# Gated graph kernel on one core: hx and h0 turned feature-major by a DMA trip and 32x32 vector transposes, scores from unsplit fp32

## What is computed

```python
h = jnp.maximum(_layernorm(x, axis=-1), 0.0)
x = x + _L0_gnn_ref(h, adj, Wq, Wk, Wv)        # q k^T, times adj^T, over its row norm, times v
h = jnp.maximum(_layernorm(x, axis=-1), 0.0)
# layer 1, three steps:
for _ in range(3):
    a_in = a_out = adj @ h                      # both matrices are adj here
    z = sigmoid(lin(av, w3) + lin(h, u3)); r = sigmoid(lin(av, w4) + lin(h, u3))
    hv = tanh(lin(av, w5) + lin(r * h, u5))
    h = (1 - z) * h + z * hv
x = x + h
```

## Time and profile before

| what | us |
|---|---|
| median of 3 runs (lowest, highest) | 1010.53 (1009.56, 1012.95) |
| the profiled execution | 1010.0 |
| its span in the trace | 1008.0 |
| one round of six windows (187.34 to 309.14) | 121.80 |
| PE busy, DVE busy, ACT busy | 981.4, 660.9, 526.1 |

### The profile page before, as it was taken

How to read it: one execution, slowest core, us unless ns; L and a number is a source line. 1 busy time by engine, 2 the same in 40 slices (tenths; PEclk the granted TensorE clock), 3 DMA queues, 4 the chain that set the end, 5 groups by cost and what they waited for, 6 DMA issues and landing times.

```text
span 1008.0 us, 15357 instructions
## 1 busy us (share of the span) xinstructions
PE 981.4 (97%) x5448; PEld 850.1 (84%) x5448; DVE 660.9 (66%) x1326; ACT 526.1 (52%) x921; POOL 78.3 (8%) x90
## 2 busy tenths in 40 slices
PE   5899999999999999999999999999999999999996
PEld 4788888888888888888888888888888888888885
DVE  4865757757676665766667676676657757576645
ACT  4455554546446464554735646356554555545552
POOL 1210101101010000100001000100001101010000
PEclk9799999999999999999999999999999999999998
DMA  5010000200011000200002000010000100000001
GB/s 163 5 39 1 1 1 22 63 0 0 0 43 40 0 0 0 83 0 0 0 20 63 0 0 0 21 62 0 0 0 21 62 0 0 0 21 21 1 1 42
DMA packets 21377, 20.06 MB, mean 20 GB/s; under 512 B 2160, under 2 KB 21360, under 8 KB 21360
## 3 DMA queue, kind: packets, MB, share of 16 engines
q1 hardware_dynamic: 21360, 19.83, 6.1%
HBM read 11.44 MB, written 8.39 MB: 20 GB/s over the span
## 4 chain that ended last, share of the span: by engine, by line
PE 92%; DVE 4%; ACT 1%; issue 1%; DMA 0%; SPq 0%; POOL 0%; DVEq 0%
PE gate L311 13%; PE gate L313 13%; PE gate L312 13%; PE fea L414 8%; PE cand L311 8%; PE cand L312 8%; PE cand L313 8%; PE tok L407 4%; PE fea L372 2%; PE tok L311 2%; PE tok L313 2%; PE tok L312 2%; PE tok L346 1%; PE fea L311 1%; PE fea L313 1%; PE fea L312 1%
## 5 line engine op out<-in xcount | busy, mean ns | idle before, releaser
L672 ACT ACTIVATE r_s<-gate,b_r 128x512 f32<-128x512 f32 x96 | 64.9, 685 | 103.1 <-PE gate L313 103.1
L828 DVE TENSOR_TENSOR d_s<-c_s,h 128x512 f32<-128x512 f32 x96 | 64.2, 688 | 61.9 <-ACT c_s L691 61.9
L828 DVE TENSOR_TENSOR a_lo<-fea,a_hi 128x512 fp32r<-128x512 f32 x96 | 65.4, 688 | 44.0 <-ACT a_hi L603 44.0
L691 ACT ACTIVATE c_s<-cand,b_c 128x512 f32<-128x512 f32 x96 | 64.4, 689 | 51.3 <-PE cand L313 51.3
L828 DVE TENSOR_TENSOR rh_lo<-rh,rh_hi 128x512 fp32r<-128x512 f32 x96 | 66.7, 735 | 32.9 <-ACT rh_hi L603 30.7
L950 DVE TENSOR_TENSOR rh<-r_s,h 128x512 f32<-128x512 f32 x96 | 64.9, 689 | 34.8 <-ACT r_s L672 34.8
L603 ACT ACTIVATE h_hi<-h 128x512 fp32r<-128x512 f32 x64 | 39.5, 633 | 87.6 <-DVE h L944 87.6
L603 ACT ACTIVATE a_hi<-fea 128x512 fp32r<-128x512 f32 x96 | 57.4, 599 | 49.6 <-PE fea L414 49.2
L311 PE MATMUL gate<-a_hi,W_hi_wz 128*128 128x512 f32 x192 | 79.3, 413 | 0.0
L311 PE MATMUL cand<-a_hi,W_hi_w 128*128 128x512 f32 x192 | 78.7, 410 | 0.0
L311 PE MATMUL cand<-rh_hi,W_hi_u 128*128 128x512 f32 x192 | 77.6, 404 | 0.0
(11 more groups left out here) (116 smaller groups left out, 2348.1 us busy)
## 6 DMA issues: line engine op xcount, KB each, us to landing
x_s<-x SPq DMA_DIRECT2D x16, 512.0 KB, 4.4
out<-o_s SPq DMA_DIRECT2D x16, 512.0 KB, 3.0
z_s<-w_t SPq DMA_DIRECT2D x1, 512.0 KB, 4.2
r_s<-w_t SPq DMA_DIRECT2D x1, 512.0 KB, 5.1
c_s<-w_t SPq DMA_DIRECT2D x1, 512.0 KB, 6.1
rh<-u_t SPq DMA_DIRECT2D x2, 256.0 KB, 6.4
d_s<-wq SPq DMA_DIRECT2D x1, 256.0 KB, 3.8
d_s<-wk SPq DMA_DIRECT2D x1, 256.0 KB, 4.0
```

The lines of the kernel that those rows point to most:

```text
L672: nc.scalar.activation(r_s[:, c, :], gate[:, c, :], ACT.Sigmoid, bias=b_r[:, c:c + 1]).then_inc(r_ready, 1)
L691: nc.scalar.activation(c_s[:, c, :], cand[:, c, :], ACT.Tanh, bias=b_c[:, c:c + 1]).then_inc(c_ready, 1)
L828: return nc.vector.tensor_tensor(dst, a, b, ALU.subtract)
```

## The change

In the rounds the transposes of `hx` and of `h0` on PE go. SP writes the tile to a DRAM scratch and reads it back as four DMAs of 32 partitions, so that 32x32 blocks stand where they belong, and DVE turns the blocks (`turn`). `hxT` and `h` then lie in SBUF, and the splits read from there. For this `normalise` writes `hx` and `h0` in another order of columns; `adjacency` on `h0` reads its weights from it with a step of 8 elements (32 bytes). The start keeps the transposes on PE (the old functions get the suffix `_start`) and there ACT copies `hxT` as well. Scores everywhere are one plain fp32 matmul of `hxT` and the unsplit q, which DVE copies (`take_q`), so `split_q`, `take_S_aside` and the addition of the halves go. `queries` moves in windows 2 (from before `transpose_state`) and 4 (from the end of window 3) to the place behind `candidate_a`, and `scores` behind `values`.

```diff
         hx = sb("hx", [P, Q, D])
+        hx_back = sb("hx_back", [P, BL, Q, C, K])
+        hxT = sb("hxT", [P, C, T])
         hxT_hi = sb("hxT_hi", [P, C, T], f32r)
         hxT_lo = sb("hxT_lo", [P, C, T], f32r)
-        q_s = sb("q_s", [P, 2, C, T], f32r)
-        q_hi, q_lo = q_s[:, 0, :, :], q_s[:, 1, :, :]
+        q_s = sb("q_s", [P, C, T])
         v_hi = sb("v_hi", [P, Q, D], f32r)
         v_lo = sb("v_lo", [P, Q, D], f32r)
...
 
-        feaA = fea[:].rearrange("p c (a h n) -> p (c a) h n", h=2, n=P)
...
+        hx_trip = nc.dram_tensor("hx_trip", (2, P, Q * D), f32, kind="Internal").ap()
+        h0_trip = nc.dram_tensor("h0_trip", (2, P, Q * D), f32, kind="Internal").ap()
+
+        hx_b = hx[:].rearrange("p q d -> p (q d)").rearrange("p (b q c f) -> p c b f q", b=BL, q=Q, c=C)
+        h0_m = [t[:].rearrange("p q d -> p (q d)").rearrange("p (m q c) -> p m q c", q=Q, c=C) for t in h0]
...
+            def blocks_back(back, trip, done):
+                for b in range(BL):
+                    sp.dma_start(back[b * K:(b + 1) * K].rearrange("t a x y z -> t a (x y z)"),
+                                 trip.rearrange("(a t) (b x) -> b t a x", t=K, b=BL)[b]).then_inc(done, 16)
+
+            def turn_hx(g, s):
+                sp.wait_ge(hx_ready, Q * (g + 1))
+                sp.dma_start(hx_trip[s], hx[:].rearrange("p q d -> p (q d)")).then_inc(hx_out, 16)
+                sp.wait_ge(hx_out, 16 * (g - 1))
+                blocks_back(hx_back, hx_trip[s], hx_in)
...
+                turn_hx(2 * i + 2, 0)
+                turn_hx(2 * i + 3, 1)
+                turn_h0(2 * i + 2, 0)
                 store(2 * i, 0, use_in_round("final 5", i))
+                turn_h0(2 * i + 3, 1)
                 store(2 * i + 1, 1, use_in_round("final 0", i))
...
-            def scores(g, n, n_q):
-                pe.wait_ge(q_hi_ready, 2 * g + 2)
+            def scores(n, n_q):
                 pe.wait_ge(fea_taken, 2 * n_q + 2)
                 fea_wait(n, 0)
                 fea_wait(n, 1)
                 for q in range(Q):
                     for c in range(C):
-                        nc.tensor.matmul(feaA[:, q, :, :], hxT_hi[:, c, graph_pair(q)], q_s[:, :, c, graph_pair(q)],
-                                         start=c == 0, stop=False, skip_group_check=True)
-                        last = nc.tensor.matmul(feaA[:, q, 0, :], hxT_lo[:, c, graph_pair(q)], q_hi[:, c, graph_pair(q)],
-                                                start=False, stop=c == C - 1, skip_group_check=True)
+                        last = nc.tensor.matmul(feaS[:, q, :], hxT[:, c, graph_pair(q)], q_s[:, c, graph_pair(q)],
+                                                start=c == 0, stop=c == C - 1)
                 last.then_inc(fea_full, 2)
...
-            def adjacency(c, src, n):
+            def adjacency(c, src, n, in_blocks=False):
 
                 fea_wait(n, c)
                 for q in range(Q):
-                    last = nc.tensor.matmul(fea[:, c, graph_pair(q)], src[:, q, c * P:(c + 1) * P], adjT[:],
-                                            start=True, stop=True)
+                    state = src[:, :, q, c] if in_blocks else src[:, q, c * P:(c + 1) * P]
+                    last = nc.tensor.matmul(fea[:, c, graph_pair(q)], state, adjT[:], start=True, stop=True)
...
                 if k == 1:
-                    tok_done(use_in_round("new 0", i - 1))
+                    pe.wait_ge(h_lo_new, 4 * i + 4)
                     reset_gate(w, s, use_in_round("adj 0", i - 1))
...
                     candidate_a(w, s)
                     adjacency(1, t_s, use("adj 1"))
                     candidate_rh(w, s)
-                    if attention:
-                        transpose_hx(2 * i + 2, use("split x X"))
...
                     pe.wait_ge(h_lo_ready, 8 * i + 2)
                     reset_gate(w, s, use("adj 1"))
-                    if attention:
-                        queries(2 * i + 2, use("q X"), use("split x X"))
...
                     candidate_rh(w, s)
                     if attention:
                         norms(2 * i + 2, use("norm X"))
@@ -503,11 +531,7 @@
                     adjacency(0, t_s, use("adj 3"))
                     adjacency(1, t_s, use("adj 3"))
...
                         pe.wait_ge(h0_ready, Q * (2 * i + 3))
-                        transpose_new(2 * i + 2, o, use("new 5"))
-                        adjacency(0, h0[o], use("adj 5"))
+                        adjacency(0, h0_m[o], use("adj 5"), in_blocks=True)
                     candidate_a(w, s)
                     if new:
-                        adjacency(1, h0[o], use("adj 5"))
+                        adjacency(1, h0_m[o], use("adj 5"), in_blocks=True)
                     candidate_rh(w, s)
                 else:
-                    tok_done(use("new 5"))
+                    pe.wait_ge(h_lo_new, 4 * i + 2)
                     reset_gate(w, s, use("adj 5"))
                     transpose_state(w, o, use("final 0"))
                     update_gate(w, s)
                     pe.wait_ge(h0_ready, Q * (2 * i + 2))
-                    transpose_new(2 * i + 1, o, use("new 0"))
-                    adjacency(0, h0[o], use("adj 0"))
+                    adjacency(0, h0_m[o], use("adj 0"), in_blocks=True)
                     candidate_a(w, s)
-                    adjacency(1, h0[o], use("adj 0"))
+                    adjacency(1, h0_m[o], use("adj 0"), in_blocks=True)
                     candidate_rh(w, s)
 
...
                 act.wait_ge(shift_ready[n], g + 1)
                 dst, done = (hx, hx_ready) if n == 0 else (h0[s], h0_ready)
+                dst_b = hx_b if n == 0 else h0_b[s]
                 for q in range(Q):
-                    nc.scalar.activation(dst[:, q, :], x_s[s][:, q, :], ACT.Relu, bias=shift[n][:, q:q + 1],
+                    out, src = dst[:, q, :], x_s[s][:, q, :]
+                    if in_blocks:
+                        out = dst_b[:, :, :, :, q]
+                        src = src.rearrange("p (c b f) -> p c b f", c=C, b=BL)
+                    nc.scalar.activation(out, src, ACT.Relu, bias=shift[n][:, q:q + 1],
                                          scale=rstd[n][:, q:q + 1]).then_inc(done, 1)
...
+            def split_new(g, s):
+                for c in range(C):
+                    act.wait_ge(h_new_ready, 2 * g + (c + 1))
+                    copy(h_hi[s][:, c, :], h[s][:, c, :]).then_inc(h_hi_ready, 1)
...
+                        normalise(1, 2 * i + 3, 1, in_blocks=True)
                 else:
                     reset_sigmoid(w)
                     split_rh(w)
-                    split_new(o, use("new 0"))
                     update_sigmoid(w)
                     split_a(o, 0, use("adj 0"))
                     split_a(o, 1, use("adj 0"))
+                    split_new(2 * i + 1, o)
                     candidate_tanh(w)
 
...
+            def turn(dst, back, c):
+                return nc.vector.transpose(dst[:, c, :].rearrange("p (q a t) -> p a q t", q=Q, a=BL), back)
+
+            def turn_hx(g):
+                dve.wait_ge(hx_in, 16 * BL * (g - 1))
+                for c in range(C):
+                    turn(hxT, hx_back[:, :, :, c, :], c).then_inc(hxT_turned, 1)
+
+            def split_hx(g):
+                for c in range(C):
+                    dve.wait_ge(hxT_hi_ready, 2 * g + (c + 1))
+                    sub(hxT_lo[:, c, :], hxT[:, c, :], hxT_hi[:, c, :]).then_inc(hxT_lo_ready, 1)
+
+            def take_q(n):
                 for c in range(C):
                     fea_wait(n, c)
-                    dve.wait_ge(q_hi_ready, 2 * g + (c + 1))
-                    sub(q_lo[:, c, :], fea[:, c, :], q_hi[:, c, :]).then_inc(fea_taken, 1)
+                    nc.vector.tensor_copy(q_s[:, c, :], fea[:, c, :]).then_inc(fea_taken, 1)
...
-            def mask_scores(g, n):
+            def mask_scores(n):
                 fea_wait(n, 1)
-                dve.wait_ge(S_aside_ready, g + 1)
-                nc.vector.tensor_tensor(S_sum[:], feaA[:, :, 0, :], S_aside[:], ALU.add).then_inc(fea_taken, 2)
-                dve.wait_ge(fea_taken, 2 * n + 2)
...
+            def turn_h0(g, s):
+                dve.wait_ge(h0_in, 16 * BL * (g - 1))
+                for c in range(C):
+                    turn(h[s], h0_back[:, :, :, :, c].rearrange("p a f q -> p a q f"), c).then_inc(h_new_ready, 1)
+
+            def split_new(v, s):
+                for c in range(C):
+                    dve.wait_ge(h_hi_ready, 2 * v + (c + 1))
+                    sub(h_lo[s][:, c, :], h[s][:, c, :], h_hi[s][:, c, :]).then_inc(h_lo_new, 1)
...
                     split_state(w, o)
+                    if attention:
+                        turn_hx(2 * i + 2)
                     reset_state(w, s)
+                    if attention:
+                        split_hx(2 * i + 2)
                     split_rh(w)
...
@@ -1041,26 +1087,28 @@
                     dve.wait_ge(h_new_ready, 4 * i + 2)
```

(73 more changed lines are left out.)

93 lines of the change are left out of this document (46 added, 47 removed).

## The result

The changed kernel takes 1030.86 us (median of 4 runs, 1030.55 to 1032.23) against 1010.76 us before, ratio 1.0204 with a 95% interval of 1.0187 to 1.0221: 20 us slower, where 18 us faster was forecast. The profiled execution took 1030.55 us with a span of 1028.8.

What follows compares the result with a forecast made beforehand. PE, busy 121.29 of 121.80 us in a round, was taken as the bound: 1010.0 - 24.4 (transposes) - 3.5 (v_lo waits) + 10.2 (round-end stall) = 992.3, say 992 us; range 984 to 1015.

Steps and rivals of the forecast that it cites:

- What bounds the kernel, and what leaves PE: In the rounds PE bounds the time; removing transposes of hx and h0 for 14 groups saves 24.4 us.
- waits for v_lo: At the weighted sum PE waited 0.5 us seven times; splitting v ahead of the mask saves 3.5 us.
- The strided weights: Adjacency products on h0 load fp32 columns 32 bytes apart; taken as 0, upper bound 22.4 us at double the time.
- Turns on DVE: Each 128x512 turn on DVE takes 0.68 us, like a copy of that size; upper bound 0.95.
- rival (2): Only the turns of h0 are slow, 1.2 instead of 0.6 us; r*h of window 5 0.3 late: 1002.8; 8%.
- rival (1): Strided loads of h0 bind PE: 1014.7 at double time, otherwise 997 to 1013; 33%, half of it near double.
- The new stall at a round's end: PE waits 1.45 us before reset_gate of window 1 for DVE's second h_lo, seven times: +10.2 us.
- The trip of hx: DRAM write and four reads of X's hx take 8.2 us (6.5 to 11.7); cost 0 up to 11.2 us.
- Scores: Eight plain fp32 products take 1.62 to 1.70 us plus 0.08 surcharge, against 1.80 before; difference taken as 0.
- The start: ACT's extra copies add 0.8 us before the first queries, a shorter scores-to-norms way returns it: 0, 1 us either way.
- SP's queue: SP's output stores now stand behind the h0 trip of X and the four h0 reads of Y; cost nothing.
- The chances: Probabilities against the kernel before: faster 0.73, slower 0.15, same 0.12, with 0.3% (3 us) as the threshold.

Runs made afterwards that it cites:

- e_dense_order: Changed kernel with h0 written twice by ACT (adjacent columns for the products) and the new state's turns and splits ahead of the second adjacency split: 983.01 us, 0.9716.
- b_step2: Kernel before the change, with only h0 stored so that the columns of a weight load lie 2 elements (8 bytes) apart: 1012.44 us.
- b_step4: Kernel before the change, with only h0 stored so that the columns of a weight load lie 4 elements (16 bytes) apart: 1036.50 us.
- c_dense: Changed kernel, own order, ACT writing h0 twice: adjacent columns for the products, hx's column order for the trip, so no 32-byte steps: 994.36 us, 0.984.
- d_dense_slow_turn: Changed kernel with h0 written twice, adjacent columns for the products, the trip's copy in the changed column order, so turns keep 32-byte steps: 1006.89 us, 0.9955.
- b_step8: Kernel before the change, with only h0 stored so that the columns of a weight load lie 8 elements (32 bytes) apart: 1039.39 us.

## Why the prediction was wrong, point by point

**What bounds the kernel, and what leaves PE** held. PE's time is the result's time: e_dense_order shows it at 500.00 of 500.00 us, and the 24.4 us of transposes plus the 3.5 us of waits for v_lo came off (forecast 982.9 for these two alone from 1010.8, measured 983.01). That it fits to 0.1 us is partly luck: in the traces the seven rounds lost 29.7 us, 1.8 more than these two, and the first round began 2.2 us later.

**"The strided weights. ... I take 0"** is the step that failed, and the costliest: 24.9 of the 38.6 us between forecast and result. The upper bound stood in the text (22.4 us, "at double the time"), 2.5 us under what was measured. The reason for taking 0 was wrong: that PE reads its moving operand at 512 columns in 0.23 us says how fast it reads adjacent elements, and nothing about elements 16 bytes or more apart. b_step2 and b_step4 show that the price begins between 8 and 16 bytes. These products were already paced by their loads, so all of the longer load showed.

**"Turns on DVE ... I take the copy's 0.68"** was right for hx (687 ns) and for h0 without the stride (685 in c_dense), and wrong for h0 as changed (1143). That was rival (2), held at 8% as if it were apart from rival (1). Both come from one thing, the step of 32 bytes in h0, and they came together: the two should have been one case, 992.3 + 22.4 + 10.5 = 1025.2, above the range. The late r*h of window 5, which rival (2) had at 0.3 us, is seen at 0.2 in d_dense_slow_turn; in the changed kernel the longer product calls hide it.

**The new stall at a round's end** was right in mechanism and place and, with dense turns, in size (10.2 us forecast, 10.2 in c_dense, if without the 0.2 us beside each wait). As changed it was 16.2, the slower turns making up the difference.

**The clock** was left out. The forecast priced a wait at its own length; after waits of 2.3 us, in every second round, eight matmuls at half clock came on top, 6.5 us. With it the joined case gives 1031.7, against 1030.86, but that is partly luck: the loads cost 24.9 instead of 22.4 us, the slow turns 6.0 instead of 10.5.

**The trip of hx** cost nothing, as forecast: issued at 204.94, the write lands 2.6 us later and the last read 2.9 us after an issue at 208.9; DVE reaches its turn at 213.60 and waits for no DMA. By those numbers it takes some 6.9 us, where I counted 8.2. **Scores** at 0 were right to 1.2 us in all: the 16 records of the new form run from 227.43 to 229.14, 1.71 us, plus the surcharge. **The start** cost 1.0 us, as much as the forecast allowed. **SP's queue** cost nothing that can be seen.

**The chances** were added up wrongly: by its own parts, "faster" was 0.45 + 0.08 + 0.07 + 0.05 + 0.11 = 0.76, not 0.73. And the range ended just above rival (1) alone, so no case with two of the costs together was inside it.

## What to carry to other kernels

A layout made to suit a transfer has to be priced again at every engine that reads it: here an fp32 load with columns 16 or 32 bytes apart took about twice as long, and a turn that reads in steps of 32 bytes 1.7 times, while a load with columns 8 bytes apart cost nearly nothing more (0.85 us a call instead of 0.81). Two costs with one cause belong in one case, with one chance. When work moves behind another hand-off on an in-order engine, count the chain from its last input to the reader: here two lines in another order were worth 24 us, more than the waits themselves, since after some of the waits of 2.1 to 2.35 us the clock fell too.

## What the hardware showed unasked

- Transposes on PE whose weights lie 32 bytes apart run at the old pace (0.88 us for 8 in b_step8, 0.87 before), while plain fp32 products with the same weights need 1.70 to 1.82 us instead of 0.81.
- After a wait of 2.14 to 2.35 us PE's level fell for eight matmuls (0.42 us each instead of 0.23) in four of seven rounds of the changed kernel, after one of 2.32 in three of seven of d_dense_slow_turn, and not after other waits of the same length; after the waits of 1.49 in c_dense never.
- ACT's write of h0 in steps of 32 bytes took 847 ns instead of 589 for 128x256 (b_step8, where all 64 writes go in such steps, against the kernel before); no run shows it on the path.
